# A fused four-layer graph network on one core: four kept adjacencies, folds by transposition, written-out orders for the first and last rounds

## The reference

```
x = x + chebyshev(h, adj)      # L = I - D adj D; polynomials to order 3, four 64x64 weights
x = x + attention_net(h, adj)  # encode to 128, two attention layers (q, k, v, scores * mask
                               #   - NEG * (1 - mask), softmax, values), three-layer MLP
x = x + relu(D' (adj + I) D' (h @ W))                            # graph convolution
t = adj @ h;  x = x + where(t > 0.5, 1, 0 * t)                   # the last layer
```

## Time and profile before

| | before |
|---|---|
| runs | 814.39, 815.5, 816.0 us, median 815.5 |
| the profiled execution | 816.79 us, of which the span is 814.7 us |
| PE busy | 754.9 us, 93% |
| DVE busy | 542.0 us, 67% |
| ACT, POOL busy | 425.8 and 364.7 us |
| mean granted clock of TensorE | 0.982 |
| HBM traffic | 37 GB/s over the span |

### The profile page before, as it was taken

One profiled execution on the slowest core, in us unless ns is written; L12 is line 12 of the kernel. 1 busy time (PEld: TensorE's weight loads), 2 busy tenths in 40 slices (PEclk: granted clock), 3 DMA queues, 4 the chain that ended last, 5 costly groups with the idle time before them and its releaser, 6 DMA issues.

```text
span 814.7 us, 11514 instructions
## 1 busy us (share of the span) xinstructions
PE 754.9 (93%) x3752; PEld 531.3 (65%) x3752; DVE 542.0 (67%) x1631; ACT 425.8 (52%) x897; POOL 364.7 (45%) x492
## 2 busy tenths in 40 slices
PE   8787999999999999999999999999999999999745
PEld 4455676767776676767767676776667676775523
DVE  3765668577767858687776857776785768774521
ACT  3163837455572836556482745557283655546310
POOL 4253544354455435355454435446553535542200
PEclk9998999999999999999999999999999999999995
DMA  6100203002020302103020201203020210001010
GB/s 183 44 10 5 72 14 77 15 20 72 1 80 13 77 14 44 48 8 84 0 79 14 79 14 20 72 8 81 5 79 13 43 50 8 26 0 21 14 19 6
DMA packets 38539, 31.22 MB, mean 38 GB/s; under 512 B 24656, under 2 KB 26192, under 8 KB 38480
## 3 DMA queue, kind: packets, MB, share of 16 engines
q1 hardware_dynamic: 37488, 30.26, 14.7%
q10 hardware_dynamic: 992, 0.23, 0.1%
HBM read 28.32 MB, written 2.16 MB: 37 GB/s over the span
## 4 chain that ended last, share of the span: by engine, by line
PE 64%; DVE 23%; issue 5%; ACT 3%; DMA 2%; POOL 2%; POOLq 0%; SPq 0%; DVEq 0%; ACTq 0%
PE pre_ps L1039 8%; PE post_ps L1039 8%; PE turn_ps L1164 7%; PE turn_ps L1156 5%; PE qkv_ps L1107 4%; PE qkv_ps L1112 4%; PE post_ps L1056 3%; PE score_ps L1141 3%; PE score_ps L1142 3%; PE score_ps L1138 3%; DVE h_t L887 2%; PE pre_ps L1056 2%; PE pre_ps L998 2%; PE pre_ps L1007 2%; PE post_ps L1173 2%
## 5 line engine op out<-in xcount | busy, mean ns | idle before, releaser
L655 ACT ACTIVATE negz<-negz,negmax 128x512 f32<-128x512 f32 x128 | 92.5, 722 | 116.4 <-DVE negmax L873 115.9
L1164 PE MATMUL turn_ps<-pt,v_n 128*128 128x512 f32 x256 | 117.7, 602 | 1.0 <-ACT pt L662 1.0
L614 ACT ACTIVATE y_t_pre<-pre_ps 128x512 f32<-128x512 f32 x48 | 28.7, 597 | 137.5 <-PE pre_ps L1039 137.5
L865 DVE TENSOR_TENSOR score_ps<-score_ps,a_nat 128x512 f32<-128x512 f32 x128 | 89.0, 695 | 15.8 <-PE score_ps L1142 14.7
L873 DVE CUSTOM_DVE_ANT_0 negz<-score_ps,gate 128x512 f32<-128x512 f32 x128 | 88.5, 692 | 4.8 <-POOL gate L535 0.5
L1039 PE MATMUL pre_ps<-at_hi,u_pair_pre 128*128 128x512 f32 x192 | 85.8, 447 | 3.1 <-DVE u_pair_pre L792 2.6
L464 POOL TENSOR_TENSOR rstd_pre<-vareps_pre,nhalf 128x4 f32<-128x4 f32 x32 | 35.3, 1102 | 116.6 <-DVE vareps_pre L754 115.1
L541 POOL TENSOR_TENSOR q_lo<-q_t,q_hi 128x512 fp32r<-128x512 f32 x32 | 40.8, 1275 | 100.2 <-ACT q_t L632 100.2
L1039 PE MATMUL post_ps<-at_hi,u_pair_post 128*128 128x512 f32 x128 | 61.2, 478 | 26.1 <-DVE u_pair_post L792 26.1
L1164 PEld LDWEIGHTS turn_ps<-pt,v_n 128*128 128x128 f32 x256 | 46.1, 190 | 57.5 <-issue 45.9
L464 POOL TENSOR_TENSOR rstd_post<-vareps_post,nhalf 128x4 f32<-128x4 f32 x32 | 36.0, 1125 | 96.1 <-DVE vareps_post L754 96.0
(11 more groups left out here) (155 smaller groups left out, 1690.2 us busy)
## 6 DMA issues: line engine op xcount, KB each, us to landing
a_nat<-in_adj SPq DMA_DIRECT2D x15, 1024.0 KB, 5.9
inv_row<-inv_d SPq DMA_DIRECT2D x32, 256.0 KB, 4.1
x_in<-in_x SPq DMA_DIRECT2D x16, 128.0 KB, 2.2
out<-x_out SPq DMA_DIRECT2D x16, 128.0 KB, 1.9
a_nat<-in_adj SPq DMA_DIRECT2D x4, 256.0 KB, 4.7
inv_d<-inv_total SPq DMA_DIRECT2D x32, 2.0 KB, 1.6
cheb_ws<-in_L_gnn_weight ACTq DMA_DIRECT2D x2, 64.0 KB, 3.5
att_w<-in_L_gnn_a_wv SPq DMA_DIRECT2D x2, 64.0 KB, 3.9
```

The lines of the kernel that those rows point to most:

```text
L655: sc.activation(probs[:, i, :], negz[:, i, :], ACT.Exp, bias=negmax[:, i:i + 1], scale=-1.0, accum_out=total[:, i:i + 1]).then_inc(probs_d ...
L865: ve.tensor_tensor(score_ps[i % 2][:], score_ps[i % 2][:], a_nat[s][:, i, :], ALU.mult)\
L1164: mm = te.matmul(turn_ps[0][:], v_n[a][:, j * P:(j + 1) * P], pt[:, j, :], start=(j == 0), stop=(j == RB - 1))
```

## The change

What it does:

- The transposed halves and `dinv` are kept for four graphs (`g.keep = n % 4`) instead of three. `a_nat`, `x_in` and `x1` stay at three. The order may now have five ages, 0 to 4, and the vector and scalar lists begin at another point of the same cycle.
- `cheb_fold2`, `cheb_fold1` and `last_fold` use `turn_up`: four transpositions instead of four float32 matmuls. High and low halves then stand side by side, and DVE adds them. `cheb_fold2` has one more DVE operation, `cheb_fold1` two, `last_fold` two. Two of POOL's three operations of `cheb_f0` are gone; `roots` has two more of 4 elements.
- Rounds 0 to 2 (`HEAD`) and the last five (`TAIL`) have lists of their own; `ORDER` covers rounds 3 to 15.
- For the first and the last graph (`by_dma` false) the inverse goes by PE and ACT: `spread_inv` transposes `inv_total` broadcast along 128 columns, `copy_inv` copies it. `by_column` lets the values product follow each transposed block, and puts it in a bank of its own.
- The last graph has 19 and 20 matmuls of no use ahead of `gcn_prop` and `last_prop`.
- The bias rows are set up with fewer and wider operations, in entries of their own; `mask_bias` waits for the adjacency itself and in `HEAD` stands before `roots`.

The diff, cut to its core; the lists are shown by a line each, and by their instructions below.

```diff
@@ ORDER["tensor"] @@
-        turn1.2-2 turn2.2-2 queries.1-1 turn_a0-0 turn3.2-2 turn_a1-0 keys.1-1 attend.2-2
+        scores0.2-2 turn_a0-0 turn_a1-0 scores1.2-2 queries.1-1 scores2.2-2 turn_a2-0 turn0.2-2
...
@@ graph_layers @@
-        at_hi = [sb(f"at_hi{s}", [P, RB, N], F32R) for s in range(SLOTS)]
-        at_lo = [sb(f"at_lo{s}", [P, RB, N], F32R) for s in range(SLOTS)]
+        at_hi = [sb(f"at_hi{s}", [P, RB, N], F32R) for s in range(KEEP)]
+        at_lo = [sb(f"at_lo{s}", [P, RB, N], F32R) for s in range(KEEP)]
...
+        def by_dma(g):
+            return 0 < g.n < B - 1
+        def by_column(g):
+            return g.n in (0, B - 1)
+        def pv_bank(g):
+            return post_ps[:] if first(g) else pre_ps[:, 1, :] if by_column(g) else turn_ps[0][:]
+        def half(ps, a):
+            return ps.rearrange("p (i a c) -> p i a c", a=2, c=C)[:, :, a, :]
...
+            def turn_up(t, ready, bank):
+                pe.wait_ge(y_copied[t], ready)
+                for i in range(RB):
+                    mm = te.transpose(bank[:, i * P:(i + 1) * P], y_t[t][:, i * P:(i + 1) * P], ident[:])
+                return mm
...
+            def attend_column(g, a, i):
+                pe.wait_ge(pt_copied, 8 * g.n + 4 * a + i + 1)
+                if i == 0:
+                    pe.wait_ge(qkv_done, 10 * g.n + 5 * a + 5)
+                for j in range(RB):
+                    mm = te.matmul(pv_bank(g)[:, i * P:(i + 1) * P], v_n[a][:, j * P:(j + 1) * P],
+                                   pt[:, j, i * P:(i + 1) * P], start=(j == 0), stop=(j == RB - 1))
+                return mm
+            def spread_inv(g, a):
+                if by_dma(g):
+                    return
+                pe.wait_ge(inv_done, 2 * g.n + a + 1)
+                pe.wait_ge(pt_copied, 8 * g.n + 4 * a + 4)
+                for i in range(RB):
+                    mm = te.transpose(turn_ps[1][:, i * P:(i + 1) * P],
+                                      inv_total[:, i:i + 1].to_broadcast([P, P]), ident[:])
+                mm.then_inc(inv_ready, 1)
...
@@ cheb_fold1, DVE @@
-                dve.wait_ge(f0_done, g.n + 1)
+                dve.wait_ge(diff_done, g.n + 1)
+                dve_pre.add(ve.scalar_tensor_tensor(tmp[:], tmp[:], 2.0, half(pre_ps[:, 1, :], 0),
+                                                    ALU.mult, ALU.add))
                 dve.wait_ge(dve_pre.sem, dve_pre.so_far())
-                dve_pre.add(ve.tensor_tensor(tmp[:], rows(pre_ps[:, 1, :]), over_blocks(d_neg[:]), ALU.mult))
+                dve_pre.add(ve.tensor_tensor(tmp[:], half(pre_ps[:, 1, :], 1), tmp[:], ALU.add))
                 dve.wait_ge(dve_pre.sem, dve_pre.so_far())
+                dve_pre.add(ve.tensor_tensor(tmp[:], tmp[:], over_blocks(d_neg[:]), ALU.mult))
...
+            IDLE_AT_END = {"gcn_prop": 19, "last_prop": 20}
+            def keep_busy_at_end(g, step):
+                if g.n == B - 1:
+                    pe.wait_ge(biased, 8 * B)
+                    spare(IDLE_AT_END[step])
```

More of the change, by code:

```diff
@@ L45 @@
-    "scalar": """
[L46 to L50, removed]
@@ L51 @@
-    "vector": """
[L52 to L56, removed]
+        scores0.2-2 turn_a0-0 turn_a1-0 scores1.2-2 queries.1-1 scores2.2-2 turn_a2-0 turn0.2-2
@@ new lines @@
+        turn_a3-0 scores3.2-2 keys.1-1 turn1.2-2 cheb_ht-0 last_prop-3 values.1-1 cheb_weights-0
+        last_fold-3 turn2.2-2 scores0.1-1 cheb_prop3-0 turn3.2-2 scores1.1-1 cheb_fold3-0
+        spread_inv.2-2 attend.2-2 cheb_prop2-0 scores2.1-1 turn0.1-1 cheb_fold2-0 mlp1-2
+        turn1.1-1 scores3.1-1 mlp2-2 cheb_prop1-0 mlp3-2 turn2.1-1 turn3.1-1 cheb_fold1-0
+        spread_inv.1-1 attend.1-1 gcn_prop-2 queries.2-1 gcn_fold-2 enc_ht-0 keys.2-1 encode-0
+        values.2-1""".split(),
+    "scalar": """
+        mlp1-3 copy_pt1.1-2 mlp2-3 row_sum0-0 exp3.1-2 cheb_copy1-1 copy_pt2.1-2 copy_pt3.1-2
+        row_sum1-0 copy_inv.1-2 gcn_copy-3 queries.2-2 enc_ht-1 keys.2-2 row_sum2-0 row_sum3-0
+        encode-1 values.2-2 copy_at0-0 copy_at1-0 exp0.2-2 queries.1-1 copy_at2-0 exp1.2-2
+        copy_at3-0 copy_pt0.2-2 keys.1-1 cheb_ht-0 copy_pt1.2-2 exp2.2-2 last_copy-3 exp3.2-2
+        values.1-1 copy_pt2.2-2 cheb_copy3-0 copy_pt3.2-2 exp0.1-1 exp1.1-1 copy_inv.2-2
+        cheb_copy2-0 exp2.1-1 copy_pt0.1-1""".split(),
@@ L57 @@
+    "vector": """
+        stats_gcn-3 cheb_fold1-1 norm_gcn-3 stats_enc-1 attend.1-2 norm_enc-1 stats_cheb-0
+        gcn_fold-3 enc_ht-1 stats_last-3 mask0.2-2 split_at0-0 split_at1-0 mask1.2-2 norm_cheb-0
+        split_at2-0 norm_last-3 split_at3-0 mask2.2-2 cheb_ht-0 mask3.2-2 cheb_weights-0
+        invert.2-2 last_fold-3 mask0.1-1 cheb_fold3-0 mask1.1-1 attend.2-2 mask2.1-1
+        cheb_fold2-0 mask3.1-1 invert.1-1 mlp3-2 bias_rows.1-0 bias_rows.2-0""".split(),
     "gpsimd": """
-        norm_enc-1 norm_cheb-0 split_qk.1-1 mask_bias-1 add_cheb_bias-0 roots-0 cheb_u3-0
@@ L932, in last_fold @@
                 dve.wait_ge(last_ready, g.n + 1)
-                dve_post.add(ve.scalar_tensor_tensor(last[:], rows(post_ps[:]), 0.5, x3[:],
+                dve_post.add(ve.tensor_copy(u2[:], half(post_ps[:], 0)))
+                dve.wait_ge(dve_post.sem, dve_post.so_far())
+                dve_post.add(ve.tensor_tensor(u2[:], half(post_ps[:], 1), u2[:], ALU.add))
+                dve.wait_ge(dve_post.sem, dve_post.so_far())
+                dve_post.add(ve.scalar_tensor_tensor(last[:], u2[:], 0.5, x3[:],
                                                      ALU.is_gt, ALU.add))
@@ L1211, in _ @@
                     scores3=scores(3), turn1=turn_probs(1), turn2=turn_probs(2),
-                    turn3=turn_probs(3), attend=attend),
+                    turn3=turn_probs(3), spread_inv=spread_inv, attend=attend),
                 **layer(1, queries=queries, keys=keys, values=values),
```

329 lines of the change are left out of this document (207 added, 122 removed).

## The result

The changed kernel takes 785.65 us (median of 4 runs, 784.45 to 787.2) beside 815.39 us for the kernel before on the same chip: a ratio of 0.964 with a 95% interval of 0.9615 to 0.966. That is 30 us less; the forecast was 40 less. The profiled execution is 786.5 us, with a span of 784.7.

What follows compares the result with a forecast made beforehand. PE's throughput bounds the kernel, 44.4 us of a 46.46 us round. Middle -21.6, last round +1, head -4, second round -3.8, tail -11.2 sum to -39.6 on 816.8: 777.2, median about 775 us, range 760 to 789.

Steps and rivals of the forecast that it cites:

- The likeliest case: Whole kernel: shorter middle, head, second round and tail give about 775 us, within 766 to 785; chance 0.52.
- Rival 2: Middle rounds: late norms feed back and waits eat the folds' gain, rounds 45.6 to 46.4, 785 to 796 us; chance 0.12.
- Rivals 3 and 5: Low clock: under the tail's matmuls of no use, 781 to 786 us, chance 0.08; in middle rounds, 823 us, chance 0.02.
- Rows by the hidden waits: Middle round: 44.4 us PE throughput, less 1.35 for folds, plus 1.7 waits, gives 44.8 us, 1.7 less than before.
- so it waits about 1.0: PE at `encode`, middle round: DVE's split ends at 11.9 us, PE arrives at 10.8, a new wait of about 1.0.
- The visible 1.15 us goes: PE ahead of `last_prop`, middle round: the 1.15 us wait for DVE's `u_pair_post` disappears, as `last_prop` comes a round later.
- Folds: Three folds a graph: four transpositions take 0.43 us for four matmuls' 0.89, saving 0.45 each, 1.35 us a round.
- The head, -4: From first to second keys, 42.8 us before: the new list fills half of eight us of waits, -4 (0 to -7).
- The second round, 42.7: Second round: no `last_prop` and fold, 0.43 for `spread_inv`, so 42.7 us for 46.5, -3.8.
- The tail, -11.2: From the last keys to the end, three pieces: -1.0 to `queries.2`, -6.0 to `mlp1`, -4.2 to the end.
- Rival 4: Middle: SP's `store` holds layer 2's inverse 2.3 us, delaying DVE in `attend.2` and PE behind it; slower, chance 0.02.
- a hold by the DMA: Sign of being wrong: DVE's `attend.2` held by the DMA in the middle; right meant no `inv_row` wait over 0.5 us.

Runs made afterwards that it cites:

- experiment 8: The changed kernel with POOL's difference for `q_lo` cut from 512 to 128 columns, order unaltered: 783.9 us (ratio 0.962).
- experiment 2: The changed kernel with only its three folds as float32 matmuls again, without the DVE additions: 798.15 us (ratio 0.979).
- experiment 3: The changed kernel with `cheb_fold1` alone as float32 matmuls, the other two folds transposed: 786.7 us (ratio 0.966).
- experiment 1: The changed kernel's code with the old order, DMA inverse, single product, no matmuls of no use: 837.9 us with transposed folds, 817.4 with matmul folds.
- experiment 9: The changed kernel with DVE's `enc_ht` ahead of `gcn_fold` and 14 matmuls of no use in the first graph's layer 2: 780.5 us (ratio 0.958).
- experiment 4: The changed kernel without the last graph's 19 and 20 matmuls of no use: 790.1 us (ratio 0.969).
- experiment 6: The changed kernel with SP issuing layer 2's inverse ahead of the store of the graph before: 787.2 us (ratio 0.966).

## Why the prediction was right and where it was off

The likeliest case was right in kind: faster, by the middle, the ends and the second round, with the place of the new wait. It was 10 us too hopeful, most of all by the price of one DVE operation and by the clock in the head. The 785.65 us lie just above the 766 to 785 of my own case, where the ranges of rivals 2 (from 785) and 3 (to 786) lie too, so the number alone doesn't tell them apart; the waits, the folds and the clock do, below.

- **Rows by the hidden waits: 44.4 us of throughput, less 1.35 for the folds, plus 1.7 of new waits.** The middle round is 45.17 (11 of the 13; the last two are 45.9 and 46.1, for which I had +1). The waits that show are 2.0 us and not 1.7. I had laid out 1.7 to 2.2 and kept the lower end. This is the mis-sized term, 0.3 to 0.4 us a round, some 4.4 over the 13; the two last rounds are the rest of the 5.0.
- **"The split for `encode` 0.7: 11.9 ... so it waits about 1.0".** The place was right and the wait 1.23. The step that failed is laying out DVE's new order "with row durations": `gcn_fold` was 0.9 us, from a trace in which POOL was elsewhere, and is 1.77 in the new one (342.60 to 344.37). The reorder itself put the operation beside `q_lo` (experiment 8). The wait grew by 0.23 and not by these 0.87, so the rest of my layout was too long by some 0.6.
- **"The visible 1.15 us goes."** It went to 0.27 at `last_prop`, and not to none.
- **Folds, "1.35 us" a round.** Each is 0.44 us to the next start, as said, but the three are worth 0.95 (experiment 2), because `cheb_fold1`'s share is waited for at `attend` (experiment 3). I had priced its saving and that wait apart ("`attend` waits for `copy_pt3` some 0.4"); they are the same time. And the saving is not a term by itself: without the order it is a loss of 20.5 us (experiment 1). The prediction's sum reads as if it were additive.
- **The head, -4.** It came to -1.5 with the 0.7 ahead of the first keys, so the keys of graph 1 are at 84.2 and not at 81 to 83. As far as experiment 9 shows it, the second keys lost 2.3 to 2.8 us to the clock, behind waits that I had seen in the earlier trace rows and expected the new list to fill.
- **The second round, 42.7.** It is 42.6.
- **The tail, -11.2.** It is -9.1. Its pieces are 20.1, 21.0 and 27.9 us for 19.4 (whose own terms add up to 19.3), 19.9 and 27.6. The second holds the largest miss, 1.1 of its -6.0. From `queries.2` to the second matmul of `scores0` it is 7.80 us (735.75 to 743.55), 1.0 less than in the trace of before for the -1.6 that I had, and from there to `mlp1` 13.24, 3.8 less for -4.4. No single wait answers for it; the 1.64 for POOL's `k_lo` is as long as it was. The matmuls of no use end in time (the row has 18 of the first 19, in 4.05 us, for the estimate of 4.1), and are worth 4.5 us (experiment 4).
- **Rival 4, SP holding the inverse.** Its mechanism is there: the reciprocal runs at 360.00 us and the inverse leaves at 362.36, behind the store at 361.88, 2.4 us later. DVE waits up to 1.9 us for it, more than the 0.5 that I had called right. But PE does not wait, and taking the delay away gives nothing (experiment 6), as the 1.4 us of slack behind it said. I had named a hold by the DMA as a sign of being wrong; it came, and cost nothing.
- **Slips in the text.** "The last keys near 702" doesn't follow from the sum, whose parts give 708.2 (they came at 715.7). And "the clock's last slices are down to 7, 4 and 5 tenths" takes the first two from the row of PE's busy share: the clock of the earlier trace rows has one low slice, the last. Neither is in the sum.
- **Rival 2**, waits that eat the folds, holds for one fold of three. **Rivals 3 and 5** are out: the clock is full to the end, and full through the middle with 68 transpositions a round. In the head the dip went with the waits covered and the transpositions left, and it is there in two kernels whose folds are matmuls (experiment 9), so there too the transpositions aren't what the traces point to.

What stays open: whether ACT's `k_t` is the last limit near 44.8, since both ways of relieving DVE stop there and the one try at moving ACT's work gave nothing; and in how many executions the head's dip falls (two of four by the estimate of experiment 9).

## What to carry to other kernels

Price an operation in its new place and not by its row in the old trace: look at what the other engines run at that moment, above all when a DVE operation with both operands in SBUF may come to stand beside a POOL operation. A saving on the bound engine counts only up to the next thing that this engine waits for, so one small edit can be worth -20 us in one order and +12 in another; test edits of that kind inside the order that they were made for. Where one engine is busy from end to end, its first idle microseconds at the two ends cost twice, by the wait and by the clock behind it, and matmuls of no use that fit under the wait bring the second part back.
